# Self-attention and channel grouping on one core: four of eight row tiles in hi/lo parts, spread over ACT, VectorE and GpSimd, with four tiles scored ahead

## What is computed

```python
xf  = x.reshape(B, C, N)                                   # B=8, C=128, N=1024
x_f = Wf @ xf + bf;  x_g = Wg @ xf + bg;  x_h = Wh @ xf + bh    # 16, 16, 128 channels
beta = softmax(x_f^T x_g, axis=-1)                         # 1024 x 1024 per image
y = x + gamma * (x_h @ beta)
# second layer
y_n = y / max(|y| over pixels, 1e-12)
cos = sum over images of (y_n y_n^T) / B                   # 128 x 128
idx = top_k(-|cos|.T, 4)                                   # each channel's 4 least similar channels
mean, var = moments of y over the channel and its 3 partners, per image
out = gamma2 * (y - mean) * rsqrt(var + 1e-5) + beta2
```

## Time and profile before

| | |
|---|---|
| median of 3 runs | 213.73 us (213.5 to 213.83) |
| the profiled execution's own time | 213.6 us |
| its span, first to last instruction | 211.8 us |
| mean granted TensorE clock | 0.946 of full |
| PE busy | 187.0 us, 88% of the span |
| DVE busy | 174.3 us, 82% |
| ACT busy | 144.4 us, 68% |
| POOL busy | 34.4 us, 16% |

### The profile page before, as it was taken

The page is one execution under the profiler, slowest core; times in us unless marked ns, Lnnn a source line. Parts: engine busy times, 40 slices in busy tenths (PEclk is TensorE's granted clock), DMA queues, the critical chain, the costliest instruction groups (busy, mean ns, idle before and its releaser), DMA issues.

```text
span 211.8 us, 2308 instructions
## 1 busy us (share of the span) xinstructions
PE 187.0 (88%) x727; PEld 115.9 (55%) x727; DVE 174.3 (82%) x317; ACT 144.4 (68%) x256; POOL 34.4 (16%) x39
## 2 busy tenths in 40 slices
PE   7599979999999999999999999999999999983100
PEld 2454546465765676566756675667566756371000
DVE  6678989979898889989898989888988898766650
ACT  2548976799379955995599658985799378740320
POOL 0200210034003400160007000520034001001400
PEclk9969999999999999999999999999999999996555
DMA  5880000000000000000000000000000000000198
GB/s 209 315 330 0 0 3 0 3 0 0 0 3 0 0 0 0 0 3 2 0 0 2 0 0 3 0 0 0 0 3 2 0 0 0 0 3 2 57 400 335
DMA packets 2892, 8.87 MB, mean 42 GB/s; under 512 B 320, under 2 KB 448, under 8 KB 2880
## 3 DMA queue, kind: packets, MB, share of 16 engines
q1 hardware_dynamic: 2304, 7.34, 9.0%
q10 hardware_dynamic: 576, 1.38, 1.7%
HBM read 4.52 MB, written 4.19 MB: 41 GB/s over the span
## 4 chain that ended last, share of the span: by engine, by line
PE 73%; DVE 11%; ACT 6%; issue 5%; POOL 1%; DVEq 0%; ACTq 0%; POOLq 0%
PE o_ps L602 40%; PE s_ps L583 12%; PE w_ps L572 7%; PE w_ps L577 6%; PE w_ps L617 3%; PE w_ps L611 2%; DVE nmax L376 2%; ACT probs L292 2%; PE o_ps L569 2%; DVE y_all L562 1%; DVE probs_low L390 1%; DVE g_parts L399 1%; DVE y_all L414 1%; ACT probs_high L298 1%; ACT fg_neg L285 1%
## 5 line engine op out<-in xcount | busy, mean ns | idle before, releaser
L292 ACT ACTIVATE probs<-s_ps,nmax 128x1024 f32<-128x1024 f32 x64 | 71.0, 1109 | 40.4 <-DVE nmax L376 40.2
L602 PE MATMUL o_ps<-probs,vnorm 128*128 128x512 f32 x192 | 89.9, 592 | 0.5 <-DVE y_all L414 0.5
L376 DVE TENSOR_REDUCE nmax<-s_ps 128x1 f32<-128x1024 f32 x64 | 78.0, 1220 | 12.8 <-PE s_ps L583 12.3
L583 PE MATMUL s_ps<-g_parts,f_parts 128*128 128x512 f32 x128 | 52.0, 489 | 3.8 <-DVE g_parts L399 2.2
L602 PEld LDWEIGHTS o_ps<-probs,vnorm 128*128 128x128 f32 x192 | 35.7, 189 | 28.0 <-issue 22.8
L240 POOL TENSOR_TENSOR f_parts<-fg,fg_neg 64x512 fp32r<-64x512 f32 x14 | 24.0, 1715 | 122.2 <-ACT fg_neg L285 122.2
L583 PEld LDWEIGHTS s_ps<-g_parts,f_parts 128*128 128x128 f32 x128 | 21.4, 191 | 20.1 <-issue 15.1
L390 DVE TENSOR_TENSOR probs_low<-probs,probs_high 128x1024 fp32r<-128x1024 f32 x16 | 19.5, 1220 | 1.4 <-ACT probs_high L298 1.3
L309 ACT ACTIVATE vnorm<-values,rinv 128x128 f32<-128x128 f32 x48 | 18.8, 392 | 0.0
L577 PEld LDWEIGHTS w_ps<-wd,x_all 128*128 128x128 f32 x112 | 14.7, 192 | 6.7 <-issue 6.7
L399 DVE TENSOR_TENSOR g_parts<-fg,fg_neg 64x512 fp32r<-64x512 f32 x16 | 14.0, 872 | 4.9 <-ACT fg_neg L285 4.1
(11 more groups left out here) (90 smaller groups left out, 169.2 us busy)
## 6 DMA issues: line engine op xcount, KB each, us to landing
x_all<-x_dram SPq DMA_DIRECT2D x7, 512.0 KB, 6.1
out_dram<-y_all SPq DMA_DIRECT2D x5, 512.0 KB, 5.8
out_dram<-y_all ACTq DMA_DIRECT2D x2, 512.0 KB, 4.1
x_all<-x_dram SPq DMA_DIRECT2D x2, 256.0 KB, 3.7
out_dram<-y_all SPq DMA_DIRECT2D x2, 256.0 KB, 2.2
wd<-wide_dram ACTq DMA_DIRECT2D x1, 256.0 KB, 4.3
wd<-wide_dram ACTq DMA_DIRECT2D x1, 66.5 KB, 3.4
```

Source lines behind the costliest of these rows:

```text
L292: nc.scalar.activation(probs[t][:, :], s_ps[t % 2][:, :], ACT.Exp, bias=nmax[:, t:t + 1], accum_out=rsum[:, t:t + 1]).then_inc(exp_done, 1)
L376: nc.vector.reduce_max(nmax[:, t:t + 1], s_ps[t % 2][:, :], AX_X, negate=True).then_inc(max_ready, 1)
L583: last = nc.tensor.matmul(s_ps[t % 2][:, h], f_parts[par][:, t * P:(t + 1) * P], g_parts[par][:, h], start=True, stop=True)
L602: last = nc.tensor.matmul(o_ps[:, halves[h]], weights[:, :], rows[:, halves[h]], start=(t == 0 and n == 0), stop=(t == T - 1 and n == len( ...
```

## The change

It does these things together:

- Four of eight tiles are split, not two: in the first image all but 0, 1, 2 and 4, in later ones all but 1, 4, 5 and 7 (so 0, 2, 3 and 6 are split).
- The high probabilities are made by ACT as before, one step after the tile's exp (from the second image on); the low ones by POOL (L266). The values of every tile are scaled by DVE, in a form that also writes an accumulator (L420); for a split tile ACT makes the high part (L344) and POOL the low one (L287).
- Four tiles are scored ahead, not three; in the first image a table says how many.
- f and g are no longer copied to SBUF and then added twice. ACT makes the negated high part straight from PSUM in one instruction (`negate_high`, L319), DVE adds all 128 rows in one instruction (`make_parts`, L425, also from PSUM), and a DMA of SP moves the g rows to where the f rows stand (L243).
- The works of a stage stand at other steps: residual of b-1 at the start of t = 0, f/g of b+1 at t = 0 and 1 on PE, ACT and DVE alike, all transposes in one piece at t = 2, ACT's and DVE's cut of these at t = 3, values at t = 4 and 5 on PE and DVE, the Gram product at t = 6, its scaling at t = 7, ACT's sum of squares at t = 5, POOL's inverse norm at t = 6.
- `x_all` and `y_all` are one buffer `xy`. Six probability buffers are left of eight.

The core of the diff:

```diff
-AHEAD = 3
+AHEAD = 4
 SCALED = 2
-SPLIT = (3, 7)
+PROBS = 6
+PARTS = 5
...
+WHOLE_FIRST = (0, 1, 2, 4)
+WHOLE_LATER = (1, 4, 5, 7)
+
+SCORED_FIRST = (3, 4, 6, 7, 9, 10, 11, 12)
...
+            for b in range(1, B):
+                for h in range(H):
+                    sp.wait_ge(parts_ready, H * b + h + 1)
+                    sp.dma_start(g_rows[b % 2][f_rows, halves[h]].bitcast(F32),
+                                 fg_parts[b % 2][g_part_rows, halves[h]].bitcast(F32)).then_inc(g_moved[h], 16)
...
+            for b in range(B):
+                for t in range(T):
+                    for n in newly_copied(b, t):
+                        if is_split(n):
+                            low_part(n)
+                    n = T * b + t + SCALED
+                    if n < TILES and is_split(n):
+                        low_values(n)
+                    if b > 0 and t == 6:
+                        invert_norm(b - 1)
...
+            def negate_high(b, h):
+                act.wait_ge(fg_proj, H * b + h + 1)
+                if b > 0:
+                    act.wait_ge(parts_ready, H * (b - 1) + h + 1)
+                nc.scalar.activation(fg_neg[:, halves[h]], w_ps[:, halves[h]], ACT.Identity,
+                                     bias=low_bias[:, 0:1], scale=wd[:, NMASK:NMASK + 1]).then_inc(neg_ready, 1)
...
+            for b in range(B):
                 for t in range(T):
+                    for n in newly_scored(b, t):
+                        exp(n)
+                        if b == 0 and is_split(n):
+                            high_part(n)
+                    if b > 0:
+                        for n in newly_copied(b, t):
+                            if is_split(n):
+                                high_part(n)
+                    n = T * b + t + SCALED
+                    if n < TILES and is_split(n):
+                        high_values(n)
+                    if t < 2 and b < L:
+                        negate_high(b + 1, t)
+                    if t == 3 and b > 0:
                         act.wait_ge(yT_made, b)
                         nc.scalar.activation(yT[:, :, 0:P], w_ps[:, :].rearrange("p (t c) -> p t c", c=P),
                                              ACT.Copy).then_inc(yT_high, 1)
+                    if t == 5 and b > 0:
+                        act.wait_ge(y_ready, H * b)
+                        nc.scalar.activation(squares[:, :], xy[:, b - 1, :], ACT.Square,
...
+            def scale_values(n):
+                b, t = divmod(n, T)
+                dve.wait_ge(rinv_ready, n + 1)
+                dve.wait_ge(v_ready, H * b + t // TH + 1)
+                if b > 0:
+                    dve.wait_ge(attended, n - T + 1)
+                nc.vector.tensor_scalar(vnorm[t][:, :], values[b % 2][:, t, :], rinv[:, t:t + 1], 0.0,
+                                        ALU.mult, ALU.add, accum_out=v_sums[:, t:t + 1]).then_inc(vn_ready, 1)
+            def parts(to, rows, h, done):
+                nc.vector.scalar_tensor_tensor(to, w_ps[rows, halves[h]], wd[rows, BFG:BFG + 1],
+                                               fg_neg[rows, halves[h]].bitcast(F32), ALU.add,
+                                               ALU.add).then_inc(done, 1)
+            def make_parts(b, h):
+                dve.wait_ge(neg_ready, H * b + h + 1)
+                parts(fg_parts[b % 2][:, halves[h]], slice(0, P), h, parts_ready)
...
+            for b in range(B):
+                for t in range(T):
+                    if t == 0 and b > 0:
+                        dve.wait_ge(attended, T * b)
+                        for h in range(H):
+                            residual(b - 1, h)
+                    for n in newly_scored(b, t):
+                        row_max(n)
+                    n = T * b + t + SCALED
+                    if n < TILES:
+                        invert_sum(n)
+                        scale_values(n)
+                    if t == 0 and b > 1:
+                        add_gram(b - 2, w_ps[:, BANK:BANK + P])
+                    if t < 2 and b < L:
+                        make_parts(b + 1, t)
+                    if t == 3 and b > 0:
+                        dve.wait_ge(yT_high, b)
+                        for h in range(H):
+                            low_part(slice(h * TH, (h + 1) * TH), w_ps[:, halves[h]])
+                    if t in (4, 5) and b < L:
+                        add_value_bias(b + 1, t - 4, w_ps)
+                    if t == 7 and b > 0:
+                        scale_gram(b - 1, w_ps)
...
+            def turn_y(b):
+                if b < L:
+                    pe.wait_ge(parts_ready, H * (b + 2))
+                else:
+                    pe.wait_ge(gram_added, b)
+                transposes(xy[:, b - 1, :], w_ps, range(T)).then_inc(yT_made, 1)
...
+            for b in range(B):
+                for t in range(T):
+                    for n in newly_scored(b, t):
+                        score(n)
+                    if t == 0 and b > 1:
+                        turn_gram(b - 2, w_ps[:, BANK:BANK + P])
+                    if t < 2 and b < L:
+                        next_fg(b, t)
+                    attend(T * b + t)
+                    if t == 2 and b > 0:
+                        turn_y(b)
+                    if t in (4, 5) and b < L:
+                        next_values(b, t - 4)
+                    if t == 6 and b > 0:
+                        if b < L:
+                            pe.wait_ge(v_ready, H * (b + 1) + 1)
+                        pe.wait_ge(yT_ready, H * b)
+                        gram(w_ps, range(T)).then_inc(gram_made, 1)
```

454 lines of the change are left out of this document (183 added, 271 removed).

## The result

The change made the kernel slower, by nearly a quarter:

| | before | after |
|---|---|---|
| median | 213.78 us of 4 runs (213.50 to 213.85) | 262.58 us of 4 runs (260.26 to 262.83) |
| span of the profiled execution | 211.8 us | 261.0 us |
| granted clock, mean | 0.946 | 0.931 |
| ratio, after to before | | 1.2262 (1.2191 to 1.2332) |

The account below looks back on a forecast made before the run. PE's work bound the kernel before; added waits make middle stages 27.9 us, not 22.2. Stages and tail give 211.8 + 41.6 = 253.4, and 1.8 around it: 255 us, range 237 to 268.

Parts of the forecast that it names:

- The first wait: Middle stage: PE's transposes wait for DVE's f/g parts until 10.62 us after the residual; PE alone comes at about 7.5.
- The second wait: Middle stage: value products wait 1.7 us for DVE's low half of the transposes, starting at 17.25 us, not 15.5.
- The third wait: Stage end: Gram's scaling, ahead of the residual on DVE, waits for POOL's norm (27.2 us); next residual at 27.9.
- Stages 2 to 6: Middle stages: 27.9 us each, not 22.2, with PE 21.6 of work and 6.3 of waits; five add 28.5 us.
- First stage: Image 0: residual at 41.0 us against 36.44 (+4.6), though the first score comes at about 8.5, not 10.5.
- Stage 1: The stage with no Gram to turn: 26.9 us against 21.9 (+5.0).
- Last stage and tail: Last stage 21.0 us against 17.5, tile 2 (7.7) and tile 6 (16.9) waiting for POOL; tail unchanged at 24.9.
- Port 0: Port shared by DVE and POOL: nothing charged for DVE's scalings; upper bound 4 us a stage.
- g DMA: Move of g rows: leaves at 10.6, lands at 12.8 us, before the next image's score at 13.3; costs nothing.
- PE as the bound: Rival: parts ready by PE's 7.5 us, so PE's work still sets the pace; 206 us, chance 0.09.
- only one wait: Rival: only the wait ahead of the transposes counts, a stage is 24.9 to 26.9 us; 237 to 249, chance 0.22.
- The third, the clock: Rival: PE's granted clock also falls behind gaps, 1.35 us per stretch; 263 to 271 us in all, chance 0.12.

Follow-up runs that it names:

- e1: Kernel after the change, with ACT's negation of f/g moved ahead of the exps of its step: 247.55 us.
- e2: Kernel after the change, with ACT's cut of the transposes moved to the beginning of step 3, ahead of that step's exp: 244.38 us.
- e3: Kernel after the change, with ACT's squares at step 4 and POOL's inverse norm at step 5, ahead of its low part: 255.15 us.
- e7: Kernel after the change, with DVE's scaling of the values in the plain form, without the accumulator: 260.50 us.
- e6: Kernel after the change, with POOL making only 128 of 1024 columns of each low part: 258.98 us.
- e10: Kernel after the change plus six moves within engine lists, with fewer split tiles in images 0, 1 and the last: 213.41 us, 0.9971 of the kernel before.
- e11: e10 with PE making the first half of image 1's f/g ahead of the third score: 214.04 us, 1.0014 of the kernel before.

## Why the prediction was right or wrong

- **The first wait, right.** Transposes predicted 10.62 us after the residual, measured 10.65 (111.48 - 100.83); attend 2, held by POOL, at 7.7 and 7.65. e1 shows the cause and also the cover: with the parts in time, POOL's low values hold PE for 0.95 us (1.2 was said), as they do in the kernel after itself.
- **The second wait, right.** Values predicted at 17.25, measured at 17.35; PE's gap before them 1.57 to 1.61 us in four of the stages 2 to 6 (1.7 said); e2 shows the cause.
- **The third wait, right.** The norm was to be ready at 27.2 and was at 27.28, the next residual at 27.9 and came at 28.04. e3 shows the cause.
- **Stages 2 to 6:** predicted 27.9 each. Four measured 28.03 to 28.05, and the one from 100.83 took 28.37: there POOL's low values ahead of the norm started 0.34 us later in the stage's course than in the other four, for no reason that the trace shows. Together 1.0 us too little (140.5 for five, 139.5 said).
- **First stage, wrong by 3.5 us:** 41.0 said, 44.51 measured. The term left out was the clock. Two gaps, of 2.54 us before 26.44 (an exp) and of 2.52 us before 39.39 (POOL's low values), were in the sum as waits of 2.5 and 2.6 to 3.2; what they did to PE's clock was not:

```profile
27.00:31.00 4.00, 4.00 (x12) 3.12 (x11) 2.06 (x5) 3.94 (x7) 2.31 (x1) 0.57 0.00 0
39.00:46.00 7.00, 6.61 (x20) 4.95 (x21) 3.13 (x9) 4.12 (x7) 3.77 (x5) 0.76 0.00 1
```

  These two stretches together lack 4 x 0.43 + 7 x 0.24 = 3.4 us at full clock, the last part of it in stage 1. Also the first score came at 9.84 us and not at 8.5. The two make 4.7 us where 3.5 are missing, so they are upper bounds; no run separates them.
- **Stage 1, 1.4 us too little** (28.3 measured, 26.9 said): its clock is 0.94, and 28.3 x 0.06 is 1.7, the upper bound of what that can cost. e7's stage 1 has the same wait of 2.2 us ahead of the transposes and a clock of 1.00 throughout, and takes 27.12.
- **Last stage and tail, 1.8 us too little** (213.31 to 261.0 is 47.7, 45.9 said): POOL's waits at tiles 2 and 6 were there as said (2.49 and 2.05 us). The first ended 7.63 us into the stage (7.7 said), the second at 19.09 and not at 16.9: between them the clock is 0.85 for 11.5 us, which is worth up to 1.7.
- **Sizes.** Low part 2.37 us (2.3), low values 0.457 (0.5), parts 0.749 (0.75), negation 0.77 (0.72), split attend 1.39. Port 0, g DMA 2.2 us at the median and nothing, both as said. It took 3.9 us once: in the stage from 100.83 the next image's first score came only at 115.64, 14.8 us into the stage against the 13.3 of the prediction, which the second wait took in: PE then waited 0.1 us for the cut, not 1.6.
- **The rivals.** PE as the bound (206) fell, as did only one wait. The third, the clock, gave no time in the middle stages of this trace: they stay at 1.00 with gaps of 0.9 to 1.6 us. It came in the first stage, stage 1 and the last, behind gaps of 2.1 to 2.5 us, and can be most of the 7.6 us that were missing; after's execution with a mean clock of 0.943 took 260.26 us, the three with 0.930 or 0.931 took 262.40 to 262.83. e6 shows that the rival had a sound core: where the gap of a middle stage grows to 2.56 us, the clock is down behind it in three of five. The Trainium skill (TensorE: Matmul & The Clock Gate, What's actually happening) ties the level to how busy the array has been, not to one gap; the trace doesn't contradict it, with the middle stage still 23.00 of 28.40 us busy at 1.00.

What stays open: whether f/g in one step on all engines or the hi/lo work alone would have cost the kernel of before its 22.2 us; neither was tried by itself. Why the clock falls behind a gap in one stage or execution and not in another like it. And why the first stage keeps a stretch at 1.2 GHz in e10 and e11 wherever its gap lies, so whether the split could be worth more than 0.3%; e10's three best executions were 0.8 to 0.9% under the median before.

## What to carry to other kernels

Adding up each engine's work shows what a change could save, not what it does: for every buffer that is handed round (here `w_ps`), write out one stage with the chain of engines through it, and see whether each handover comes before the owner wants the buffer. In an in-order list a short instruction on which another engine waits belongs ahead of a long one with slack; six moves of works within their lists, with not one instruction of an engine fewer, were worth 44 us of 262. Work out the first and the last stage separately: waits for POOL that were hidden or short in the middle stages stood open there, and PE could pay for a gap twice, by the wait and by the clock behind it. And read the mean clock of every run before giving a difference of 1% to an edit: two kernels here seemed 2 us apart and weren't at equal clock.

## What the runs showed of the hardware that was not expected

- PE after a wait of over 2 us ran at 1.2 GHz for some us in some places (0.57 from 27 to 31 us, 0.50 from 12 to 14 in e10) and not in others: in e6 the same wait of 2.55 to 2.57 us before the same instruction was followed by 0.72 over six us in three middle stages and by 1.00 in two, in stage 1 the same wait of 2.2 us by 0.72 (after, 54 to 60 us) and by 1.00 (e7). Waits of 0.9 to 1.6 us, in a stage with PE 81% busy, left it at 1.00.
- Executions of one kernel fell into groups by their mean clock: in e10 211.7 to 211.9 us at 0.957, 213.1 to 213.5 at 0.951 to 0.953 and 213.6 to 214.0 at 0.937 or 0.938; after the change 260.3 at 0.943 and 262.4 to 262.8 at 0.930 or 0.931. The kernel before had two such groups, about 0.946 and 0.958, with the same time.
- A plain scaling on DVE that started just behind a POOL instruction waited it out (2.34 us for 0.29), the accumulating form never did, and the stages 2 to 6 were no longer for it.
- POOL's low part of 128x1024 took 2.37 us, one of 128x128 0.46, so most of it goes with the width.
